# A four-layer graph network on one core: the softmax of the second edge stage in single steps, a ring of 19 gathered groups, and VectorE's four chains interleaved

## The reference, cut to what matters

```python
h = relu(layernorm(x))
xw = (h @ W).reshape(n, 4, 64)                       # per head
alpha = leaky_relu(a_src[src] + a_dst[dst] + a_edge) # one number per edge and head
amax = segment_max(alpha, dst)                       # over the edges of one destination
ae = exp(alpha - amax[dst])
attn = ae / segment_sum(ae, dst)[dst]
agg = segment_sum(xw[src] * attn[:, :, None], dst)   # with one self loop per node
x = x + (h + elu(agg.reshape(n, 256) @ Wp + bp')) normalised
```

## Time and profile before

| What | Value |
|---|---|
| median of 3 runs | 3519.25 us (3516.62 to 3521.51) |
| the profiled execution, its own time | 3510.65 us |
| its span in the trace | 3508.9 us |
| mean granted TensorE clock, as a share of 2.4 GHz | 0.805 |
| VectorE busy over the whole span | 2280.8 us (65%) |
| TensorE matmuls busy over the whole span | 2551.3 us (73%) |
| GpSimd busy over the whole span | 1789.0 us (51%) |

### The profile page before, as it was taken

One profiled execution on the slowest core, in us unless ns is written; L12 is line 12 of the kernel. 1 busy time (PEld: TensorE's weight loads), 2 busy tenths in 40 slices (PEclk: granted clock), 3 DMA queues, 4 the chain that ended last, 5 costly groups with the idle time before them and its releaser, 6 DMA issues. The chain is left out here.

```text
span 3508.9 us, 58176 instructions
## 1 busy us (share of the span) xinstructions
PE 2551.3 (73%) x14132; PEld 2166.8 (62%) x14132; DVE 2280.8 (65%) x5044; ACT 1062.1 (30%) x2723; POOL 1789.0 (51%) x1813
## 2 busy tenths in 40 slices
PE   3778777514554444357777765999999999999986
PEld 2778776413443333245555544888888888888872
DVE  3555555337887887855556542677777777777775
ACT  1111111134554564111111101344444344443441
POOL 2777776066666663157777723444444344443400
PEclk7776777556555666589999967999999999999985
DMA  2443443265554552035445517988888888888830
GB/s 64 93 87 84 87 87 64 46 161 131 132 123 125 132 124 72 2 110 157 153 153 161 158 63 177 203 204 197 197 201 199 200 198 190 193 200 198 195 92 9
DMA packets 433884, 475.50 MB, mean 136 GB/s; under 512 B 200837, under 2 KB 304648, under 8 KB 433712
## 3 DMA queue, kind: packets, MB, share of 16 engines
q1 hardware_dynamic: 358832, 295.60, 35.9%
q0 software_dynamic: 59904, 123.64, 15.2%
q10 hardware_dynamic: 14976, 54.53, 4.5%
HBM read 408.18 MB, written 65.34 MB: 135 GB/s over the span
## 5 line engine op out<-in xcount | busy, mean ns | idle before, releaser
L1960 PE MATMUL psum<-ckv,z 128*128 128x256 f32 x4160 | 969.7, 384 | 0.0
L1960 PEld LDWEIGHTS psum<-ckv,z 128*128 128x128 f32 x4160 | 767.9, 191 | 98.5
L1823 POOL DMA_INDIRECT ga<-XX,src_i x416 | 398.1, 957 | 449.7 <-PE psum L1941 307.0
L985 POOL DMA_INDIRECT ga<-T,src_i x416 | 431.4, 1037 | 302.3 <-issue 112.5
L275 POOL DMA_INDIRECT ga<-T,src_i x416 | 401.3, 965 | 151.7 <-issue 124.4
L275 POOL DMA_INDIRECT ga<-TA,src_i x416 | 412.4, 991 | 126.7 <-issue 126.7
L2009 DVE TENSOR_TENSOR z<-psum,shb 128x2560 f32<-128x2560 f32 x104 | 293.7, 2824 | 125.8 <-PE psum L1941 78.5
L455 PE MATMUL psum<-wre,re 128*128 128x68 f32 x832 | 213.4, 349 | 142.1 <-DVE oneT L331 82.6
L1816 POOL TENSOR_TENSOR acc<-acc,wkv 128x512 f32<-128x512 f32 x104 | 114.3, 1099 | 332.7 <-DMA wkv<-WKV 316.4
L455 PEld LDWEIGHTS psum<-wre,re 128*128 128x128 f32 x832 | 173.4, 258 | 162.9 <-issue 153.9
L2050 DVE TENSOR_TENSOR acc<-acc,psum 128x256 f32 x416 | 175.4, 422 | 120.2 <-PE psum L1932 90.9
(11 more groups left out here) (349 smaller groups left out, 4862.8 us busy)
## 6 DMA issues: line engine op xcount, KB each, us to landing
shb<-in_ea SPq DMA_DIRECT2D x104, 640.0 KB
WKV<-wkvo ACTq DMA_DIRECT2D x104, 512.0 KB
shb<-in_ea SPq DMA_DIRECT2D x104, 512.0 KB
wkv<-WKV SPq DMA_DIRECT2D x104, 512.0 KB
dl<-DL SPq DMA_DIRECT2D x312, 128.0 KB, 3.5
acc<-QW SPq DMA_DIRECT2D x416, 64.0 KB
win<-TB SPq DMA_DIRECT2D x416, 32.0 KB
ga<-T,src_i POOLq DMA_INDIRECT x832
```

Of the source, the lines that this page charges most:

```text
L985: pool.indirect_dma_start(ga[:, ring(g) + t, :], None, T1, bass.IndirectOffsetOnAxis(ap=src_i[:, g * GT + t:g * GT + t + 1], axis=0)).then ...
L1823: pool.indirect_dma_start(ga[:, (g % GR) * GT + t, :], None, XX, bass.IndirectOffsetOnAxis(ap=src_i[:, g * GT + t:g * GT + t + 1], axis=0) ...
L1960: last = pe.matmul(kv_of(k)[:, t, :], z[:, k % 2, j, t * 128:(t + 1) * 128], ckv[:, j, :], start=(j == 0), stop=(j == NZ - 1))
```

## The change

The softmax of a chunk is taken apart, so that one part stands in each step; the order of engines within a step changes; the ring of gathered rows gets five more groups, in `acc[:, 1:3]`; and some operations are done elsewhere. Step by step:

- `RG` 14 to 19, `WEIGH` 11 to 14, `SCATTER` 12 to 15.
- VectorE: `weigh`, `halve` and `message` (L1344, L1346, L1350 of before) alternate with the four additions of `add_sums`; the register loads stand behind `weigh`.
- VectorE: `half_logits` is gone. TensorE adds the three bf16 parts in PSUM, with 12 matmuls of 8 columns per group in place of 4 of 24.
- VectorE: `same` and `gap` are no longer computed per chunk; they are made once for all rows in the first set-up stage, written to memory (`SGT`) and loaded by SyncE in place of `drow`. Two operations of `carried` are folded into others.
- ScalarE copies the transposed logits out of PSUM (`rows_out`), which VectorE then reads from SBUF.
- TensorE: in each step first the softmax's product, which waits for VectorE's softmax part of the step before, then `sums`, then `logits`.
- Stage m1 loads `ytab` back from `T1` by seven DMAs on SyncE.

```diff
+        SGT = dram("SGT", [NT, 258])
...
+        rows_eq = edge_a[0:NT // GT].rearrange("p t h -> p (t h)")[:, 0:GT * 258].rearrange("p (t e) -> p t e", t=GT)
...
+                sp.wait_ge(c_dve, 15)
+                sp.dma_start(SGT.rearrange("(p t) e -> p t e", t=GT), rows_eq).then_inc(l_sg, 16)
...
+                c.link(dve.memset(rows_eq[:, :, 0:129], 1.0))
+                c.link(dve.tensor_tensor(rows_eq[:, :, 1:W], dr_f[:, :, 1:W], dr_f[:, :, 0:W - 1], ALU.is_equal))
+                c.mark(dve.tensor_scalar(rows_eq[:, :, 129:258], rows_eq[:, :, 0:129], -1.0, BIG, ALU.add, ALU.mult))
...
-        RG = 14
-        WEIGH = CG + 3
+        RG = 19
+        RA = 14
+        WEIGH = CG + 6
...
-        ga = tmp("ga1", [128, RG * GT, GW])
+        ga = tmp("ga1", [128, RA * GT, GW])
+        gb = acc[:, 1:3, :].rearrange("p a n -> p (a n)")[:, 0:(RG - RA) * GT * GW].rearrange("p (t f) -> p t f", f=GW)
...
                 def rows_load(c):
                     if c >= 2:
-                        sp.wait_ge(e1_top, c - 1)
+                        sp.wait_ge(e1_ab, c - 1)
                     for h in range(4):
-                        sp.dma_start(drow[h * CT:(h + 1) * CT, c % 2, :],
-                                     A["dst_rows"][c * CT:(c + 1) * CT, :]).then_inc(e1_dr[c % 2], 16)
+                        sp.dma_start(rows_sg[h * CT:(h + 1) * CT, c % 2, :], SGT[c * CT:(c + 1) * CT, :]).then_inc(e1_dr[c % 2], 16)
...
+                def rows_out(c):
+                    act.wait_ge(e1_T, c + 1)
+                    if c:
+                        act.wait_ge(e1_x, c)
+                    act.activation(lr[:].rearrange("p a e -> p (a e)"), lt[:, 0:256], ACT.Copy).then_inc(e1_lr, 1)
...
+                for x in range(-1, G + SCATTER + 1):
...
+                    if x % CG == 1 and soft:
+                        rows_out(c)
+                    if x % CG == 3 and soft:
                         exponents(c)
+                    if x % CG == 5 and soft:
+                        back_on_edges(c)
+                    if x + 1 < G:
+                        places(x + 1)
                     if 0 <= x - WEIGH < G:
                         one_hots(x - WEIGH)
                         loop_weights(x - WEIGH)
...
                     for t in range(GT):
-                        last = pe.matmul(bank[half % 2][:, (tiles + t) * 24:(tiles + t + 1) * 24], oneT[:, g % 2, t * W:(t + 1) * W],
-                                         win[:, g % UG * GT + t, :], start=True, stop=True)
+                        for q in range(3):
+                            last = pe.matmul(bank[c % 2][:, (t0 + t) * 8:(t0 + t + 1) * 8], oneT[:, g % 2, t * W:(t + 1) * W],
+                                             win[:, g % UG * GT + t, q * 8:(q + 1) * 8], start=q == 0, stop=q == 2)
...
+                    if x % CG == 1 and soft:
+                        logits_in_rows(c)
+                    if x % CG == 2 and soft:
+                        tops_in_rows(c)
+                    if x % CG == 4 and soft:
+                        sums_in_rows(c)
+                    if x % CG == 5 and soft:
+                        weights_on_edges(c)
+                    if x % CG == 6 and soft:
+                        carried_weights(c)
+                    if x % CG == 0 and 0 < c - 1 < NC:
+                        turned(c - 1)
+                    if x % CG == 1 and 0 < c - 1 < NC:
+                        projected(c - 1)
+                    if 0 <= x - SCATTER < G:
+                        sums(x - SCATTER)
                     if x < G:
                         logits(x)
...
+                    if new is not None:
+                        weigh(new)
+                    if old is not None:
+                        starts = bases_of(dve, old // UG, old % UG)
+                    if settled:
+                        own = bases_of(dve, (c - 1) * CG // UG, (c - 1) * CG % UG)[0]
+                    if old is not None:
+                        add_sums(old, 0, starts)
+                    if new is not None:
+                        halve(new)
+                    if old is not None:
+                        add_sums(old, 1, starts)
+                    if new is not None:
+                        message(new)
+                    if old is not None:
+                        add_sums(old, 2, starts)
+                    if settled:
+                        settle(c - 1, own)
                     if x % CG == 0 and soft:
                         logits(c)
                     if x % CG == 1 and soft:
+                        tops(c)
+                    if x % CG == 2 and soft:
                         highest(c)
+                    if x % CG == 3 and soft:
+                        sums_of_rows(c)
+                    if x % CG == 4 and soft:
                         weights(c)
+                    if x % CG == 5 and soft:
                         carried(c)
+                    if x % CG == 6 and soft:
+                        ratios(c)
+                    if x % CG == 7 and soft and c:
                         hold(c)
+                    if x % CG == 0 and 0 < c - 1 < NC:
+                        turn(c - 1)
+                    if old is not None:
+                        add_sums(old, 3, starts)
...
+        ytab = tmp("m1_y", [PN, NJ, HY])
...
+                for r, (j0, n) in enumerate(rounds(NJ, 4)):
+                    sp.dma_start(ytab[:, j0:j0 + n, :], T1.rearrange("(j p) f -> p j f", p=PN)[:, j0:j0 + n, 0:HY]).then_inc(m1_l[r], 16)
...
+                    pool.wait_ge(m1_l[r], 16)
```

160 lines of the change are left out of this document (63 added, 97 removed).

## The result

| What | Before | After |
|---|---|---|
| median of 4 runs each, on one chip | 3517.93 us (3509.2 to 3521.51) | 3476.8 us (3467.71 to 3489.57) |
| ratio of the medians | | 0.9889, 95% interval 0.985 to 0.9929 |
| the profiled execution, its span | 3508.9 us | 3480.4 us |
| stage, first gather to last addition | 711.2 to 1440.8: 729.6 us | 707.8 to 1388.4: 680.6 us |
| spacing of chunks 2 to 12 | 52.67 us | 47.86 us |

The kernel became 41 us faster; forecast were 82, within a range that reached to 37. The stage gave 49 us and began 3.4 earlier, m1 took 11 back. The two profiled spans differ by 28.5 only, since what follows m1's first part, where nothing was edited, took 12.7 us longer in the one than in the other; it varies by as much between the four executions e1 to e4 further down (2055 to 2067 us for the same code).

What follows compares the result with a forecast made beforehand. VectorE's own order of work was taken to set the pace. Loops of 43 and 43.4 us gave 44.5 a chunk: -89 for the stage, +1 set-up, +6 m1, together -82, so 3437 us against 3519.25; range 3410 to 3482.

Steps and rivals of the forecast that it cites:

- VectorE's step: VectorE's step without softmax falls from 4.00 to 2.89 us by interleaving independent operations, 8.9 us less per chunk.
- The fourth case: Rival: on VectorE, independent operations start as late as dependent ones; 50 us a chunk, 3502 us; chance 0.06.
- VectorE alone: VectorE's own work per chunk, without waiting for TensorE: 23.1 us of steps and 16.1 of softmax, 39.2 us.
- The wait for TensorE's sums: VectorE's first addition waits because TensorE does the softmax product before the sums; about 4 us lost a chunk.
- The logits' matmuls: TensorE's 12 logits matmuls in place of 4 take 0.55 us (bounds 0.28 and 0.84), hidden in its slack.
- The gather's spacing: GpSimd issues a gather every 1.355 us, bounds 1.352 and 1.40; 32 at 1.352 make 43.3 us a chunk.
- the fifth case: Rival: GpSimd's gathers stretch while VectorE is busy nearly without gap; 41.6 us per 0.1 us a gather; chance 0.05.
- The drain: From the last chunk's logits to the stage's end: 66 us, where it was 65.0.
- Set-up: Three more operations over 516 elements in set-up cost 1 us, between 0 and 2.
- m1, +6 of 3.5 to 13: Next stage's seven table loads cost 6 us: 3.5 if only the first shows, 13 if all do.
- the first case: The forecast itself: both loops near 44 us a chunk (43.5 to 46), 3437 us (3422 to 3458); chance 0.52.
- the third case: Rival: TensorE's sums run at half clock all through, 47.5 us a chunk, 3473 us; chance 0.22.

Runs made afterwards that it cites:

- e1: Changed kernel with the stage's loads of places and windows left out after the first ones; run once: 3499.02 us, unmodified kernel before 3540.65.
- e4: Changed kernel without the stage's later loads of places and windows, TensorE doing a group's sums ahead of the softmax product; run once: 3438.16 us.
- e2: Changed kernel without the stage's later loads of places and windows, weighing and halving replaced by reductions with one SBUF input; run once: 3448.59 us.
- e3: Kernel before the change, without the stage's later loads of places and windows; run once: 3531.21 us, with all loads 3540.65.
- c0_after: The changed kernel as it is, on another chip: 1.0028 of the kernel before.
- a3_narrow: Changed kernel with gathers from group 19 on fetching rows of 64 floats instead of 324; run once: 3888.29 us, kernel before 3871.88.
- d2: Changed kernel with one reduction over the four heads in place of halving and message: 1.0192 of the kernel before.

## Why the prediction was right or wrong

- **VectorE's step, 2.89 us**: right, 2.88. So was the claim it rests on, that an independent operation starts 0.08 or 0.09 before the end of the one before: 1003.76 against 1002.63 + 1.22. The fourth case is out, and with it the Trainium skill's rule as cited there; the same section says itself that an operation that is not held starts earlier, which the prediction left out.
- **VectorE alone, 39.2 a chunk**: nearly, 40.3 in e2. Part of the rest is the 0.24 us between the end of a softmax part and the addition behind it, where 0.15 was taken or nothing.
- **The wait for TensorE's sums, 4 us a chunk**: right in place and kind (0.98 and 0.99 behind a product at half clock, 1.2 forecast), too small in size: 47.4 us in the 400 of the window, 5.7 a chunk. I had let half of them run at full clock; the mean clock stayed 0.60. VectorE's loop is then 45.5 (e2), not 43.
- **The logits' matmuls**: 0.48 us for twelve, 0.55 taken.
- **The gather's spacing, 1.352 us, taken 1.355, at most 1.40: the step that failed.** It came every 1.49 us. I read two averages, VectorE nearly idle (0.950) and 80% busy (1.047), and put a straight line through them, so that a VectorE no busier could not slow a gather. But a mean over the busy share hides what the timeline shows: gathers of 0.95 and a quarter of them at 1.35. It is not how busy VectorE is that counts (76% after, 80% before), but how often, and how early, a gather starts under one of three instructions. The interleaving split them, and the gathers that start under one went from 59 of 240 to 119 of 261. I named this as the fifth case and dismissed it by the 0.10. Of the 3.4 us by which a chunk is longer than forecast (47.9 for 44.5) the gather accounts for all: 32 x 1.49 = 47.8. The wait for sums still has a part in it, since it spreads VectorE's step (e4). Eleven chunks are 37 us.
- **The drain, 66**: 69.7; the last steps wait for sums at half clock too, the last one 1.54 us. **Set-up, +1**: nothing to see; the first gather starts at 710.5 in e1 and in e3 alike.
- **m1, +6 of 3.5 to 13**: +11. The middle was taken, since part was to be hidden by the reductions; but the loads go out one behind the other at 4.24 us a round, slower than m1's work, so nearly all seven show. The upper bound was the right reading.
- **The sum**: 37 us of chunks, 4 of drain and 5 of m1, less 4 for an earlier start (chunk 1 at 791.8 for 796.2, 3.4 of it before the stage's first gather, which the change does not account for: e1 and e3 start alike) and 1 for the set-up, are the 41 by which forecast and measurement differ. The time fell between the first case and the range's upper end, with the direction and the rows named as tests (chunks, steps, ring, logits that wait for gathers, m1 released by loads) as forecast, except for the spacing. That the time lies in the range is luck: the third case came close by its number (3473), with a chunk of 47.5, but its cause, the sums, was not the bound.

Open is what the engines wait for on the four other chips, where the trace can't name it, and so what bounds the stage there.

## What to carry to other kernels

When a change lets one engine run freely, the engine next to it becomes the bound at the pace that it has then, not the one it had: read that pace as a distribution, by what the first engine runs when each of the neighbour's instructions starts, and not as a mean over a stretch. Where GpSimd issues gathers on the critical path, keep VectorE's instructions with two SBUF inputs few and in one piece, and give small independent ones with at most one SBUF input the places around them. A buffer lent to another stage has to be filled again, and the refill belongs inside the stage before.

## What the runs showed of the hardware

- An indirect DMA of 128 rows takes 0.95 us on GpSimd, whether the rows have 324 or 64 floats (c0_after, a3_narrow). If it starts under a VectorE operation of 1024 or 512 elements with two SBUF inputs, it ends 0.82 us after that operation (61 and 38 gathers of the kernel after), up to 2.14 us in all. One that writes 1024 elements but reads only one input from SBUF holds none (0.95, 77 gathers).
- A reduction of 1024 elements a partition takes 1.21 us along the row (e2) and 1.91 across it (d2).
- The kernel before took 3518 us on the chip of the result, 3541 on D and 3833 to 3880 on four others. The granted clock in the stage (860 to 1260 us) is alike, 0.57 to 0.62 in the runs on the first two and 0.54 to 0.59 on the four, but over the whole execution it is 0.80 to 0.81 against 0.74 to 0.78. The traces of the four have waits in the stage that they can't put down to anything; the cause of the difference is not shown.
